# A cross-attention and ternary feed-forward kernel: first batch's context loaded in rows, VectorE's b1 work moved back, last batch's projection and scores in three passes over 12-bit parts

## What is computed

```python
x = x + xattn(layernorm(x), ctx, Wq, bq, Wk, bk)
x = x + ffn(layernorm(x), w1, b1, w2, b2)
# xattn, per batch b of 4:
query = ctx @ Wq.T + bq              # 512 x 256 times 256 x 128
key   = ctx @ Wk.T + bk
attention = softmax(query @ key.T)   # 512 x 512
x_m   = layernorm(x) @ attention.T
# ffn:
w_ternary = clip(round(w / mean(abs(w))), -1, 1) * mean(abs(w))
h = gelu(x @ w1_ternary.T + b1)      # 512 -> 2048
out = h @ w2_ternary.T + b2          # 2048 -> 512
```

## Time and profile before

| | |
|---|---|
| runs | 312.27, 312.23, 311.51 us |
| profiled execution | 312.49 us, its span 310.7 us |
| PE busy | 303.9 us (98%) |
| DVE, ACT, POOL busy | 153.7, 143.9, 109.2 us |
| chain that ended last | PE 96%, DMA 2%, DVE 1% |
| float32 matmuls 128x512 of scores (L443) | 14.7 us busy, x32 records |

### The profile page before, as it was taken

One profiled execution on the slowest core, in us unless ns is written; L12 is line 12 of the kernel. 1 busy time (PEld: TensorE's weight loads), 2 busy tenths in 40 slices (PEclk: granted clock), 3 DMA queues, 4 the chain that ended last, 5 costly groups with the idle time before them and its releaser, 6 DMA issues.

```text
span 310.7 us, 3674 instructions
## 1 busy us (share of the span) xinstructions
PE 303.9 (98%) x1401; PEld 144.2 (46%) x1401; DVE 153.7 (49%) x295; ACT 143.9 (46%) x253; POOL 109.2 (35%) x111
## 2 busy tenths in 40 slices
PE   6799999999999999999999999999999999999996
PEld 3366544444444444444444444444444444444455
DVE  0888896764598853755308342445433003442101
ACT  2179998577723506542654604545440017762000
POOL 0276339999979960000903620000650000000000
PEclk9999999999999999999999999999999999999999
DMA  7899999674653992000032854000034100000011
GB/s 174 237 381 408 361 277 205 131 135 103 121 104 63 155 228 105 2 0 0 0 70 54 166 103 154 0 0 0 2 69 115 56 34 0 0 2 0 34 49 54
DMA packets 66706, 32.24 MB, mean 104 GB/s; under 512 B 59504, under 2 KB 60032, under 8 KB 66176
## 3 DMA queue, kind: packets, MB, share of 16 engines
q1 hardware_dynamic: 66368, 31.73, 40.4%
q10 hardware_dynamic: 320, 0.27, 0.4%
HBM read 15.21 MB, written 4.19 MB: 62 GB/s over the span
## 4 chain that ended last, share of the span: by engine, by line
PE 96%; DMA 2%; DVE 1%; SPq 0%; ACT 0%; issue 0%
PE ps_t L511 36%; PE ps_e L536 24%; PE ps_e L494 13%; PE ps_e L525 9%; PE ps_e L443 5%; PE ps_e L435 2%; PE ps_e L543 2%; PE ps_t L435 2%; DMA ctx_sb<-in_ctx 2%; PE ps_t L467 1%; PE ps_e L454 1%; PE ps_t L454 1%; SPq L247 0%; DVE ctxT L764 0%; ACT qkT L644 0%; DVE x_sb L1055 0%
## 5 line engine op out<-in xcount | busy, mean ns | idle before, releaser
L511 PE MATMUL ps_t<-x2T,w1T 128*128 128x512 f16 x512 | 112.1, 379 | 0.0
L706 ACT ACTIVATE ps_t<-ps_t,b_col 128x512 f32<-128x512 f32 x64 | 42.5, 665 | 96.6 <-PE ps_t L511 96.6
L511 PEld LDWEIGHTS ps_t<-x2T,w1T 128*128 128x128 f16 x512 | 50.1, 98 | 60.7 <-issue 0.6
L900 DVE SCALAR_TENSOR_TENSOR gT_lo<-ps_t,h_scale,gT_hi 128x512 f16<-128x512 f32 x64 | 45.1, 746 | 66.2 <-ACT gT_hi L711 66.2
L536 PE MATMUL ps_e<-w_raw,gT_hi 128*128 128x512 f16 x176 | 66.7, 379 | 0.0
L536 PE MATMUL ps_e<-w_raw,gT_lo 128*128 128x512 f16 x176 | 66.7, 379 | 0.0
L349 POOL TENSOR_TENSOR rstd<-var_eps,minus_half 128x4 f32<-128x4 f32 (+1 forms) x9 | 8.5, 947 | 99.7 <-DVE neg_mean L813 99.7
L711 ACT ACTIVATE gT_hi<-ps_t,h_scale 128x512 f16<-128x512 f32 x64 | 40.3, 684 | 0.0
L906 DVE SCALAR_TENSOR_TENSOR x_sb<-ps_e,h_unscale,x_sb 128x512 f32<-128x512 f32 x15 | 11.0, 748 | 57.9 <-PE ps_e L536 54.6
L536 PEld LDWEIGHTS ps_e<-w_raw,gT_lo 128*128 128x128 f16 x176 | 17.2, 98 | 21.4 <-issue 1.0
L536 PEld LDWEIGHTS ps_e<-w_raw,gT_hi 128*128 128x128 f16 x176 | 17.2, 98 | 21.1 <-issue 0.7
(11 more groups left out here) (86 smaller groups left out, 290.9 us busy)
## 6 DMA issues: line engine op xcount, KB each, us to landing
w_raw<-in_L_ffn_w SPq DMA_DIRECT2D x8, 1024.0 KB, 14.7
x_sb<-in_x SPq DMA_DIRECT2D x4, 1024.0 KB, 7.5
out<-x_sb SPq DMA_DIRECT2D x15, 256.0 KB, 2.6
ctx_sb<-in_ctx SPq DMA_DIRECT2D x16, 128.0 KB, 3.2
b_sb<-in_L_ffn_b SPq DMA_DIRECT2D x1, 256.0 KB, 7.2
w_raw<-w_raw SPq DMA_TRANSPOSE x16, 3.8
out<-x_sb SPq DMA_DIRECT2D x2, 128.0 KB, 1.7
x2n<-in_L_xattn_Wq ACTq DMA_DIRECT2D x1, 128.0 KB, 3.0
```

The source lines that it names most:

```text
L511: mm = nc.tensor.matmul(ps_t[t][:], w1T[:, k, j], x2T[:, b % 2, v, :, j], start=(v == 0 and j == 0), stop=(v == 1 and j == ND - 1))
L706: nc.scalar.activation(ps_t[t][:], ps_t[t][:], ACT.Gelu, scale=1.0 / LN_SCALE, bias=b1_col[:, k:k + 1]).then_inc(gelu_done, 1)
L900: nc.vector.scalar_tensor_tensor(out=gT_lo[:, k], in0=ps_t[t][:], scalar=h_scale[:, 0:1], in1=gT_hi[:, k], op0=ALU.mult, op1=ALU.subtract) ...
```

## The change

Two parts. In the head, batch 0's context is loaded by two DMAs in plain rows (128 rows x 2 tiles x 256), ahead of bq, bk and x. TensorE turns it with eight float32 transposes 128x128 into two PSUM banks, and VectorE copies each bank to `ctxT` (`copy_turned_ctx0` in the place of `turn_ctx(0)`). The projection goes half by half, key first, and ScalarE writes the first 128 columns of the query by themselves, so that the first scores tile can begin. The four later warm-up matmuls are gone. b1 is turned behind `project(1)`, `b1_columns` stands behind the maxima of batch 0 and ahead of `moments(1)`, and `total(B1)` and `scale_gelu` come much later, in batch 1's attention.

In the last batch, operands are split in two parts of 12 significant bits each (`cut` masks the lower 12 bits off, the rest is the difference), of type float32r, and the products upper x upper, upper x lower and lower x upper are summed: three matmuls where one float32 matmul was. VectorE cuts, POOL copies the upper and subtracts for the lower part of W and ctx; for query and key, VectorE subtracts and POOL copies. The product lower x lower is left out.

```diff
+                for h in range(2):
+                    sp.dma_start(ctx0_rows[:, 2 * h:2 * h + 2], rows[:, 2 * h:2 * h + 2]).then_inc(ctx0_here[h], 16)
...
-            load_ctx(0)
-            load_x(0)
+            load_ctx0()
             sp.dma_start(bqk[:, 0:1], bq.rearrange("(p a) -> p a", a=1)).then_inc(bqk_here, 16)
             sp.dma_start(bqk[:, 1:2], bk.rearrange("(p a) -> p a", a=1)).then_inc(bqk_here, 16)
+            load_x(0)
...
+            def split_W():
+                pool.wait_ge(W_cut_done, 1)
+                flat = W_parts[:].rearrange("p v s k h -> p v (s k h)")
+                nc.gpsimd.tensor_scalar(flat[:, 0], W_cut, 1.0, None, ALU.mult).then_inc(W_parts_done, 1)
+                nc.gpsimd.tensor_tensor(flat[:, 1], WT[:].rearrange("p s k h -> p (s k h)"), W_cut,
+                                        ALU.subtract).then_inc(W_parts_done, 1)
...
+                for h in range(2):
+                    pe.wait_ge(ctx0_here[h], 16)
+                    for k in range(NC):
+                        for t in (2 * h, 2 * h + 1):
+                            mm = nc.tensor.transpose(ps_t[k][:, t * P:(t + 1) * P], ctx0_columns[:, t, k], ident[:])
+                        if h == 1:
+                            mm.then_inc(ctx0T_ready, 1)
...
+            PARTS = ((0, 0), (0, 1), (1, 0))
...
+            def project_by_parts(free):
+                pe.wait_ge(W_parts_done, 2)
+                pe.wait_ge(ctx_parts_done, 2)
+                for s in range(2):
+                    free(s)
+                    for n, (u, v) in enumerate(PARTS):
+                        for k in range(NC):
+                            mm = nc.tensor.matmul(qk_bank(LAST, s)[:], W_parts[:, u, s, k], ctx_parts[:, v, k],
+                                                  start=(n == 0 and k == 0), stop=(n == 2 and k == NC - 1))
+                    mm.then_inc(qk_ready, 1)
...
+            def copy_first_qk():
+
+                for s, columns, n in ((1, slice(0, L), 1), (0, slice(0, P), 2), (0, slice(P, L), 2)):
...
+            def copy_turned_ctx0():
+                for k, done in enumerate((ctx0T_done, ctxT_ready)):
+                    dve.wait_ge(ctx0T_ready, k + 1)
+                    nc.vector.tensor_copy(ctxT[:, k], ps_t[k][:]).then_inc(done, 1)
...
-            turn_ctx(0)
-            b1_columns()
+            copy_turned_ctx0()
             moments(0)
             turn_ctx(1)
-            scale_gelu()
...
             for t in range(1, NT):
                 inverse(0, t)
+            b1_columns()
             moments(1)
...
             moments2(2, 3)
+            cut_projection()
             aggregate2(2)
             low_gelus(1, range(12, 16))
 
+            split_qk()
             result(1, 0)
```

More of the change, by code:

```diff
@@ L10 @@
 F16 = mybir.dt.float16
+F32R = mybir.dt.float32r
 U8 = mybir.dt.uint8
@@ L150, in xattn_ffn @@
         W_here, b1_here, bqk_here, ctx_here = sem("W_here"), sem("b1_here"), sem("bqk_here"), sem("ctx_here")
+        ctx0_here = [sem(f"ctx0_here{h}") for h in range(2)]
         x_here = [sem(f"x_here{b}") for b in range(B)]
@@ L204, in qk_bank @@
         def qk_bank(b, s):
-            return ps_t[s] if b in (1, EARLY) else ps_e[s]
+            if b == 0:
+                return ps_t[2 + s]
+            return ps_t[s] if b <= EARLY else ps_e[s]
         def scores_bank(b, t):
@@ L416, in _ @@
             add_b2(1)
+            split_W()
+            split_ctx()
             layernorm2(2)
+            upper_qk()
             layernorm(3)
@@ L425, in _, with first_projection @@
         def _(pe):
-            def warm_up(times):
-                for _ in range(times):
-                    nc.tensor.matmul(ps_e[0][:], gT_lo[:, 0, 0:P], gT_lo[:, 0], start=True, stop=True)
+            def first_projection():
+                for h in range(2):
[5 more added lines that the diff above has]
+                            mm.then_inc(ctx0T_ready, 1)
+                pe.wait_ge(WT_done, 1)
+                pe.wait_ge(ctx0T_done, 1)
+                for s in (1, 0):
+                    nc.tensor.matmul(qk_bank(0, s)[:], WT[:, s, 0], ctxT[:, 0], start=True, stop=False)
+                pe.wait_ge(ctxT_ready, 1)
+                for s in (1, 0):
+                    nc.tensor.matmul(qk_bank(0, s)[:], WT[:, s, 1], ctxT[:, 1], start=False,
+                                     stop=True).then_inc(qk_ready, 1)
             def project(b, free):
@@ L437, in project, with scores_by_parts @@
                     mm.then_inc(qk_ready, 1)
+            PARTS = ((0, 0), (0, 1), (1, 0))
[9 more added lines that the diff above has]
+                    mm.then_inc(qk_ready, 1)
+            def scores_by_parts(tiles, free):
+                pe.wait_ge(qk_upper_done, 1)
+                pe.wait_ge(qk_lower_done, 1)
+                for t in tiles:
+                    free(t)
+                    for n, (u, v) in enumerate(PARTS):
+                        mm = nc.tensor.matmul(scores_bank(LAST, t)[:], qk_parts[:, u, 0, t * P:(t + 1) * P],
+                                              qk_parts[:, v, 1], start=(n == 0), stop=(n == 2))
+                    mm.then_inc(scores_ready, 1)
             def scores(b, tiles, free):
-                pe.wait_ge(qkT_done, 2 * b + 2)
+                pe.wait_ge(qkT_done, 2 * b + 3 if b else 2)
                 for t in tiles:
@@ L548, in _ @@
             pe.wait_ge(zeros_done, 1)
-            warm_up(WARM_UP)
+            for _ in range(WARM_UP):
+                nc.tensor.matmul(ps_e[0][:], gT_lo[:, 0, 0:P], gT_lo[:, 0], start=True, stop=True)
             pe.wait_ge(ident_done, 1)
@@ L557, in _ @@
             mm.then_inc(WT_ready, 1)
[L558 to L564, removed]
+            first_projection()
             def free(t):
-                if t == 3:
-                    pe.wait_ge(b1_col_done, 1)
+                if t == 1:
+                    pe.wait_ge(qkT_done, 3)
             scores(0, range(NT), free)
             project(1, lambda k: None)
+            pe.wait_ge(b1_here, 16)
+            nc.tensor.transpose(ps_t[2][:, 0:NF], b1_rows[:], ident[0:NF, 0:NF]).then_inc(b1T_ready, 1)
             turn_xn(0)
@@ L640, in _ @@
         def _(act):
+            def copy_first_qk():
+                for s, columns, n in ((1, slice(0, L), 1), (0, slice(0, P), 2), (0, slice(P, L), 2)):
+                    act.wait_ge(qk_ready, n)
+                    nc.scalar.activation(qkT[:, s, columns], qk_bank(0, s)[:, columns], ACT.Identity,
+                                         bias=bqk[:, s:s + 1]).then_inc(qkT_done, 1)
             def copy_qk(b):
@@ L942, in _ @@
             moments2(0, 2)
-            abs_rows(W1)
             residual(0, 3)
@@ L946, in _ @@
             aggregate2(0, (2, 3))
+            abs_rows(W1)
+            low_x2(0, (0, 1))
             quantiser_scale(W1, ps_t[3])
-            low_x2(0, (0, 1))
             turn_ctx(2)
```

89 lines of the change are left out of this document (68 added, 21 removed).

## The result

The changed kernel took **316.49 us** (median of 4 runs, 315.85 to 317.28), the kernel before 312.25 (4 runs, 311.51 to 312.34). The ratio is 1.0142 with an interval of 1.0112 to 1.0173: slower by 4.2 us, where the forecast was 310.8, faster by 1.4. The profiled execution took 315.85, its span 314.1 us.

The account below looks back on a forecast made before the run. TensorE was taken to bound the run almost alone. Head -0.8, passes -1.7 and the wait for the splits +1.1 gave -1.4 us, from the median 312.23 to 310.8; own range 310.2 to 311.5, wider range 309.4 to 312.6.

Parts of the forecast that it names:

- the cost of the splits: Ahead of the last batch's projection: POOL's four operations make TensorE wait 1.0 to 1.1 us, bounds 0.4 and 1.9.
- each 0.2 dearer: Upper bound for the last batch's splits: each operation costs 0.2 us more than priced, making TensorE's wait 1.9 us.
- rival 5: Head: transposes instead of matmuls leave the clock at 1.2 GHz for the projection, 3.4 us more there, 314.2; chance 0.05.
- five rivals: The whole kernel's cases: as worked out 310.8, waits eat nearly all 312.0, little waits 309.5, two-pass float32r 316.0, head clock 314.2.
- head, at `hidden(0)`: Head: first scores start 2.3 us sooner, attention 1.0 sooner, and 0.8 us is left at `hidden(0)`.
- passes, at full clock: Last batch's projection and scores: 24 float32r matmuls at 0.216 us replace 8 float32 ones, 5.18 against 6.87, 1.7 less.
- rival 4: Last batch: float32r takes two passes, 0.43 us a matmul, total 316.0, slower; chance 0.11, with four passes (326) in it.
- by that too the sum is 1.7 less: Last batch's passes: the skill's reduced form, 4-byte values cut to 22 bits, was taken to support the 1.7 us saving.
- the wait for `xn0_read`: Head: TensorE waits some 0.7 us near 22.9 for VectorE's low part of xn, ahead of batch 1's scores.
- The piece with the two totals: Head, behind the start of `attend(0)`: an extra total and a wait for `abs_rows` cost 0.1 to 0.2 us more.
- Rival 2: Waits eat nearly all: head's gain ends in VectorE's `moments(1)`, splits cost 1.7 us, total 312.0; chance 0.24 with milder forms.

Follow-up runs that it names:

- e5: The kernel before with only the head's edits, plus eight unused POOL probe operations (one-step multiply, two-step multiply-and-add, subtraction) in POOL's idle stretch: 312.36 us.
- e8: The changed kernel with POOL's three multiplies by one written in two steps (times one, plus zero): 312.08 us against 312.16 for the kernel before.
- e9: The changed kernel with 12 unused float16 matmuls ahead of TensorE's wait for the splits: 314.61 us against 312.16 for the kernel before.
- e1: The kernel before with only the head's edits, the last batch in whole float32 without splits: 312.51 us against 312.19.
- e2: The kernel before with only the last batch's splits and three passes, without the head's edits: 315.08 us against 312.16.
- e6: The kernel before with the head's edits, b1 turned right behind the context's transposes and b1_columns ahead of moments(0): 311.11 us against 312.16.
- e3: The changed kernel with VectorE's cuts moved earlier, so that POOL splits in its idle stretch: 311.62 us against 312.19 for the kernel before.
- e4: The changed kernel with splits and wait kept, but whole float32 projection and scores behind them, parts unused: 317.10 us against 312.19 for the kernel before.

## Why the prediction was wrong

**The step that failed is the cost of the splits.** The prediction had "TensorE waits 1.0 to 1.1", with bounds of 0.4 and 1.9; it measured 3.21, beyond the upper. The sum behind it (0.75 + 1.23 + 1.12 + 2.4) went wrong in its two multiplies alone, 1.86 and 2.76. I priced an instruction with one step from the nearest rows, which have two, and set the bound ("each 0.2 dearer") around that choice instead of around what the trace left open. The subtraction was at hand as a row of POOL with another form: 1.23 for 512. A bound at the subtractions' price for the multiplies too (1.23 and 2.4) would have taken in 1.76 of the 2.75 missed. e5 shows the form's price, and e8, with nothing but the form changed, that it makes 2.59 of the 3.21.

**The clock behind the wait was missing.** The prediction weighed a fall of the clock in the head (rival 5) and nowhere else, and priced a wait on TensorE at its length. None of the five rivals holds what happened. e9 gives this term 1.55 in the chain. With it the sum by the prediction's own steps is, against what the profiled execution shows:

| | predicted | measured |
|---|---|---|
| head, at `hidden(0)` | -0.8 | -0.31 |
| passes, at full clock | -1.7 | -0.69 - 0.67 = -1.36 |
| wait for the splits, with 0.24 for the first piece behind it | +1.1 | +3.45 |
| clock behind the wait | 0 | +1.57 |
| sum | -1.4 | +3.35 |

**The passes** went as said: three of them, one pass for each float32r product, not two (rival 4) and not four. Only the size was off: 0.229 instead of 0.216 a matmul. The Trainium skill (FP8 and Floating Point Precision, TensorE Precision Notes) speaks of a reduced form that reads 4-byte values cut to 22 bits. It gives that form no price and doesn't say whether float32r is it, so the "by that too the sum is 1.7 less" of the prediction went further than the page; what is measured is 0.229 against float32's 0.86, near one of four passes. The 316.0 of rival 4 is near the measured 316.49 by chance: its mechanism did not happen.

**The head**: the mechanism was right and its size off. `scores(0)` started at 11.68 (11.4 forecast), the wait for `xn0_read` was 0.6 (0.7), VectorE's low part began at 22.66 (22.2), `attend(0)` at 28.91 (28.4). b1's work lay in VectorE's path, as the prediction had it and priced it; but the path began later, b1's transpose took 0.18 and its four operations 0.65 (0.1 and 0.55 forecast), and that carried through to `attend(0)`. In the records `attend(0)` is 29.37 - 28.91 = 0.46 sooner instead of 1.0. The piece with the two totals takes 0.35 where one total took 0.21, the 0.1 to 0.2 of the forecast. 0.46 - 0.14 is the 0.31 of the table, to rounding. In this execution VectorE stood idle for only 0.47 us ahead of b1's work (1.60 in e1, where VectorE was done sooner and TensorE later):

```profile
19.01 0.17 DVE L977 COPY b_col<-ps_t 128x16 f32<-128x16 f32 x1 [0.47 <-PE ps_t L657]
```

**What the gain was counted from** was not steady either. The 13.73 of the earlier trace rows comes from an execution whose context took 5.64 us; the same head started `scores(0)` at 12.35 in e2. In the nine profiled executions with the new head and the late b1 it starts at 11.28 to 12.39, and `hidden(0)` at 58.71 to 59.94, on average at 59.34, against 59.32 and 58.20 for the two with the old head. So the 0.31 is within what the start varies, and e1's 12 runs show no gain. That b1's place held it back is shown by e6. Rival 2, the loss of the head's gain in `moments(1)`, is what happened there, although its time of 312.0 was missed for the splits.

**Rival 5** did not come: between 4 and 10 us, with transposes in the place of matmuls, the granted clock was 1.00. The Trainium skill (TensorE: Matmul & The Clock Gate, Part 4) says that transposes don't count as busy for the full clock; this trace shows no fall from them in the head, where they ran from 5.3 to 6.9 us. The same page's table in "Why this matters for your kernels" warns of idle gaps between bursts of matmuls, behind which the clock is low again. At the place where I had not looked, this agrees in part: behind the gap of 3.2 us it fell in 19 of 25 executions.

## What to carry to other kernels

Price an instruction from a row of the same form, the number of its arithmetic steps included (a POOL multiply with an added zero cost less than half of one without), and where none is there, let the bound reach to the dearest row of that engine. A wait on a TensorE that has been working without a gap costs more than its length where the clock falls behind it; price it with and without, and if it can't be removed, try matmuls in it: here 12 float16 ones kept the clock in 4 of 4 executions. Work whose operands are ready early belongs in the idle stretch of its engine (here 30 us of POOL's), and where an engine's list is moved up, look for the one item in it that now waits for something late. And before a start is counted from one trace, look at how much it varies: a second execution with the same head began its scores 1.4 us sooner.

## What the runs showed of the hardware that was not expected

- POOL: multiply by one of 128x1024 float32 takes 2.77 us as a one-step instruction, 1.05 us with an added zero, whatever the output's type of the two; a subtraction of two tensors 2.36 (all e5). In place, 128x512 with one step took 1.86 (1.49 as a probe) and 0.99 with two, and query and key's 128x1024 took 3.81 with one and 2.08 with two (the changed kernel, e8).
- A float32r matmul of 128x512 takes 0.229 us at full clock, 0.013 more than a float16 one (e3).
- Behind the same wait of 3.2 us the clock fell in 19 of 25 executions, for half speed over 3.4 us (mean clock 0.995; the windows above) or, by the mean of 0.989, over some 0.011 x 315.4 / 0.5 = 7 us. The first cost 1.57 us in the chain and 1.7 between e4's runs. Behind waits of 0.6 to 1.1 us it fell in none of the 12 executions of e1, the 12 of e3 and the 12 of e8.
- VectorE's 12-bit cut (an integer mask) takes 0.69 us for 1024 elements and 0.41 for 512, where the float16 operation that it was priced from took 0.43.
